# Both borders of the experts' stage: a first shared tile inside attention's tail, layer 1's first rows and products ahead of the stage's end

## The reference

```python
xn = layernorm(x)
x = x + attention(xn) + experts0(xn)        # 16 heads of 16, causal; then layer 0's experts
xn = layernorm(x)
x = x + recurrence(xn) + experts1(xn)       # layer 1

def experts0(x):                            # 8 routed experts (256 -> 352 -> 256), top 2, and a shared one
    expert = lambda x, w1, b1, w3, b3, w2, b2: silu((x @ w1 + b1) * (x @ w3 + b3)) @ w2 + b2
    scores = softmax(x @ gate_w.T)
    rw = the scores of the two best of scores + gate_b, zero elsewhere
    return sum over e of rw[:, e] * expert(x, expert e) + expert(x, shared)

def recurrence(x):
    z = sigmoid(x @ Wz + bz); h_tilde = x @ Wh + bh
    h[t] = (1 - z[t]) * h[t-1] + z[t] * h_tilde[t]
    return sigmoid(h @ Wg + bg) * h

def experts1(x):
    scores = sigmoid(x @ gate.T)            # two best of the better group, normalised
    lat = x @ fc1_w.T                       # width 128, 8 experts on it
    return fc2(sum over chosen e of score * relu2(lat @ w1[e].T) @ w2[e].T) + relu2(x @ up_w.T) @ down_w.T
```

## Time and profile before

| | |
|---|---|
| median of 3 runs | 1202.05 us (1201.46 to 1204.6) |
| the profiled execution | 1203.08 us, of it 1201.3 us span, 1.78 us around it |
| mean granted clock of the matrix engine | 0.979 |
| matrix engine busy | 1115.7 us (93%), 8899 instructions |
| VectorE busy | 894.9 us (74%) |
| ScalarE busy | 676.0 us (56%) |
| GpSimd busy | 531.2 us (44%) |

### The profile page before, as it was taken

One profiled execution on the slowest core, in us unless ns is written; L12 is line 12 of the kernel. 1 busy time (PEld: TensorE's weight loads), 2 busy tenths in 40 slices (PEclk: granted clock), 3 DMA queues, 4 the chain that ended last, 5 costly groups with the idle time before them and its releaser, 6 DMA issues. The chain is left out here.

```text
span 1201.3 us, 26766 instructions
## 1 busy us (share of the span) xinstructions
PE 1115.7 (93%) x8899; PEld 747.5 (62%) x8931; DVE 894.9 (74%) x2219; ACT 676.0 (56%) x1464; POOL 531.2 (44%) x743
## 2 busy tenths in 40 slices
PE   6799999999999888998999999997999999999998
PEld 3345555555555437887998888983656646546555
DVE  5878797888887847975656667674886876877876
ACT  2355565565555554665656566654654654664653
POOL 6442433434333226854444343323646546447414
PEclk9799999999999999999999999997999999999999
DMA  6448435455334405755332453452241341331211
GB/s 162 108 90 227 99 68 110 98 98 107 62 85 93 82 18 186 218 162 155 113 101 79 126 159 122 127 155 74 89 141 35 107 140 35 105 106 63 95 45 62
DMA packets 105044, 129.36 MB, mean 108 GB/s; under 512 B 14976, under 2 KB 92736, under 8 KB 103936
## 3 DMA queue, kind: packets, MB, share of 16 engines
q1 hardware_dynamic: 93712, 109.08, 34.1%
q0 software_dynamic: 6912, 18.88, 5.6%
q10 hardware_dynamic: 4336, 0.34, 0.3%
HBM read 84.70 MB, written 43.38 MB: 107 GB/s over the span
## 5 line engine op out<-in xcount | busy, mean ns | idle before, releaser
L544 ACT ACTIVATE p<-bank 128x384 f32<-128x384 f32 (+1 forms) x384 | 191.6, 531 | 185.2 <-PE bank L957 136.1
L769 DVE TENSOR_REDUCE neg_max<-bank 128x1 f16<-128x384 f32 (+3 forms) x352 | 219.7, 640 | 65.9 <-PE bank L945 56.5
L463 POOL TENSOR_SCALAR_AFFINE_SELECT p<-p 128x256 f32<-128x256 f32 x256 | 104.5, 412 | 233.8 <-ACT p L544 233.1
L942 PE MATMUL bank<-k_stack,q_stack 96*128 96x384 f16 (+3 forms) x512 | 133.2, 312 | 23.4 <-DVE neg_max L769 13.0
L1404 POOL DMA_INDIRECT fetched<-xn_dram,token_now x80 | 81.2, 1014 | 42.9 <-POOL token_now L1400 30.7
L2033 POOL TENSOR_TENSOR up_lo<-up_sq,up_hi 128x512 f16<-128x512 f32 x32 | 43.8, 1398 | 120.8 <-ACT up_hi L2090 120.8
L2044 POOL TENSOR_TENSOR he_lo<-he_sq,he_hi 128x512 f16<-128x512 f32 x64 | 79.9, 1270 | 36.6 <-ACT he_hi L2133 36.6
L957 PE MATMUL bank<-q_stack,k_stack 97*128 97x512 f16 (+1 forms) x256 | 91.5, 360 | 3.1 <-ACT p L544 1.5
L1488 ACT ACTIVATE a<-xbank,b 128x256 f32<-128x256 f32 (+1 forms) x126 | 58.7, 469 | 52.3 <-PE xbank L151 48.8
L1576 DVE TENSOR_TENSOR h_lo<-h,h_hi 128x256 f16<-128x256 f32 x159 | 68.0, 431 | 24.3 <-ACT h_hi L1497 23.4
L975 PE MATMUL bank<-p,v_aug 128*32 128x512 f32 (+3 forms) x1024 | 83.9, 447 | 0.8 <-DVE o_rows L749 0.8
(11 more groups left out here) (344 smaller groups left out, 3379.9 us busy)
## 6 DMA issues: line engine op xcount, KB each, us to landing
w_bc<-wT_dram SPq DMA_DIRECT2D x8, 2048.0 KB, 8.3
y_routed_dram<-y SPq DMA_DIRECT2D x37, 256.0 KB
w<-in_w SPq DMA_DIRECT2D x10, 704.0 KB
pack<-in_pack SPq DMA_DIRECT2D x12, 342.0 KB, 4.4
xr<-in_x SPq DMA_DIRECT2D x8, 512.0 KB, 6.9
xn_dram<-xn SPq DMA_DIRECT2D x8, 512.0 KB, 3.0
qk_hi_dram<-qk_hi SPq DMA_DIRECT2D x16, 256.0 KB, 2.7
qk_lo_dram<-qk_lo SPq DMA_DIRECT2D x16, 256.0 KB, 2.9
```

Source lines behind the costliest of these rows:

```text
L463: pool.affine_select(out=diagonal, in_=diagonal, pattern=[[0, 2], [1, P]], compare_op=ALU.is_ge, fill=0.0, base=0, channel_multiplier=-1). ...
L544: act.activation(p32[:, s // GH % 2, s % GH, cols], s_bank[n][:, 0:cols.stop - cols.start], ACT.Exp).then_inc(p_exp.sem, 1)
L769: dve.tensor_reduce(neg_max[:, g % 2, 0:GH * TT].rearrange("p (h t) -> p h t", t=TT)[:, heads[0]:heads[-1] + 1, j], a_bank[c % 2][:, 0:len ...
L942: pe.matmul(to[:, at * w:(at + 1) * w], q_stack[0:STK, u, h0 + h, j * P:(j + 1) * P], k_stack[0:STK, u, h0 + h, 0:w], start=at == 0, stop= ...
```

## The change

In the experts' stage, `HEAD_TILES` is 10 now and `TAIL_TILES` 6. The table is made after tile 7, and the parts of `pack` are 11 of 747 columns.

At attention's end: GpSimd's iotas run at step 14 of the last batch, VectorE's slot finding at its steps 26, 28, 30 and 32. The last group's `values` go to a bank of their own (`bank[3]`), straight behind those of the group before. The transposes of the first half of the output (c = 0) stand in step 40. Gate and up of the first shared tile for m = 0 and m = 1 (24 products) stand between the steps of the tail and behind it, so that in the stage tile 0 has only m = 2; ScalarE loads silu's table there. Buffers and banks are shared by the stages.

In the experts' stage: `pack_lo` is made by GpSimd, five parts ahead of its wait for the table, four after its last fetch and two after the gather of layer 1's first rows. At the end the first sums are made one stage earlier counted from the end's sixth tile, ScalarE normalises after stage 4's hidden values, and the transposes follow `out(4)` in stage 5. The new `tail` makes, before the border, the router's products, `lat` and `z0` of layer 1's first batch, the sigmoid and `lat_hi` on ScalarE, and GpSimd's gather for batch 1. Layer 1's three small loads (biases) are issued at the stage's start.

```diff
-TAIL_TILES = 5
+TAIL_TILES = 6
+PACKED_EARLY = 5
+AT_LAST_T, AT_NUMBERS, AT_SLOTS = 40, 14, (26, 28, 30, 32)
...
+        def out_of(g):
+            return bank[3] if g == GROUPS - 1 else out_bank
...
+            first_bias(0)
+            out_high(NB - 1, 1, last_t[1])
+            act.activation(silu_table[:, :], bq[:, 0:1], ACT.Silu)
...
+                    if b + 1 == NB:
+                        if at in AT_SLOTS:
+                            find_slots(AT_SLOTS.index(at))
+                        if at - 1 == AT_LAST_T:
+                            last_high()
+                            out_low(b, 0, last_t[0])
...
+                    elif at == AT_LAST_T:
+                        pe.wait_ge(x1_ready.sem, x1_ready.at(NB - 2))
+                        out_transposes(b, 0, last_t[0])
...
-            turn_out(GROUPS - 2)
+            pe.wait_ge(a_max.sem, a_max.at(GROUPS - 1))
             for ks in AT_VALUES.values():
                 values(GROUPS - 1, ks)
+            turn_out(GROUPS - 2)
+            first_tile(0, 0)
             turn_out(GROUPS - 1)
-            for c in range(DC):
-                out_transposes(NB - 1, c, last_t[c])
-            for g in range(2):
-                out_products(NB - 1, g, last_out[g])
+            first_tile(0, 1)
+            out_transposes(NB - 1, 1, last_t[1])
+            last_products(0)
+            last_products(1)
+            first_tile(1, 0)
+            first_tile(1, 1)
...
+            def pack_part(n):
+                cols = bass.ds(n * PACK_PART, PACK_PART)
+                pool.wait_ge(pack_hi_s.sem, pack_hi_s.at(n))
+                pool.tensor_tensor(pack_lo[:, cols], pack32[:, cols], pack_hi[:, cols], ALU.subtract).then_inc(pack_lo_s.sem, 1)
...
-            pool.wait_ge(slots.sem, slots.at(0))
...
+            for n in range(PACKED_EARLY):
+                pack_part(n)
             end = pool.value_load(bounds[0:1, E:E + 1], min_val=MIN_TILES, max_val=ROUTED_TILES)
...
+            for n in range(PACKED_EARLY, HEAD_TILES - 1):
+                pack_part(n)
             pool.wait_ge(front.slot_s.sem, front.slot_s.at(0))
...
+            for n in range(HEAD_TILES - 1, PACK_PARTS):
+                pack_part(n)
...
+            pool.wait_ge(front.x2_sum.sem, front.x2_sum.at(0))
+            pool.wait_ge(front.slot_s.sem, front.slot_s.at(1))
+            for t in range(TT):
+                for k in range(2):
+                    pool.indirect_dma_start(front.rows_k[:, t, k, :], None, dram["y_routed"], ...
...
-                if stage == TAIL_TILES - 1:
-                    first_normalise()
                 for m in range(HM):
                     hidden(i, m)
+                if stage == TAIL_TILES - 2:
+                    first_normalise()
+                if stage == TAIL_TILES - 1:
+                    first_x_high()
...
-                elif stage == TAIL_TILES - 3:
+                if stage == TAIL_TILES - 4:
                     first_sums(0)
                     first_sums(1)
-                elif stage == TAIL_TILES - 2:
+                elif stage == TAIL_TILES - 3:
                     first_sums(2)
                     first_sums(3)
...
-                gate_up(i, u, 0, n)
-                gate_up(i, u, 1, n)
+                if not is_int(i, 0):
+                    gate_up(i, u, 0, n)
+                    gate_up(i, u, 1, n)
...
+            def tail(i, u):
+                out(i, u)
+                first_products(i)
```

More of the change, by code:

```diff
@@ L195, in mix_phase @@
         xn = sb("xn", [P, TT, D])
[L196 removed]
+        xT_hi, xT_lo = (carried.xT[:, k] for k in range(2))
         qk_hi, qk_lo = (sb(f"qk_{k}", [P, 4, S], F16) for k in ("hi", "lo"))
@@ L224, in mix_phase @@
         tot = sb("tot", [P, 2, TT, E])
-        run = route["run"]
-        bank = [ps(f"bank{i}", [P, 512]) for i in range(8)]
+        run, bounds, pos, slots = route["run"], route["bounds"], route["pos"], carried.slots
+        steps, above, tiles, ends, starts = carried.steps, carried.above, carried.tiles, carried.ends, carried.starts
+        base, posf, pos_part = carried.base, carried.posf, carried.pos_part
+        bank = carried.bank
         w_loaded = sig("w_loaded", 16 * 8)
-        wqkv_hi_s = sig("wqkv_hi_s", DC)
-        wqkv_lo_s = sig("wqkv_lo_s", DC)
-        w_hi = sig("w_hi", 2)
-        w_lo = sig("w_lo", 2)
+        w_hi = sig("w_hi", 4)
+        w_lo = sig("w_lo", 4)
         bq_scaled = sig("bq_scaled", 1)
@@ L497, in _ @@
                             x_bias(b + 2)
+                    if b + 1 == NB and at == AT_NUMBERS:
+                        numbers()
         @block.scalar
@@ L2035, in step @@
             def step(b, u, before, more):
-                if more:
+                if before and more:
                     gather(b + 1)
```

408 lines of the change are left out of this document (245 added, 163 removed).

## The result

The changed kernel is slower: a median of 1210.17 us (1206.92 to 1214.27, 9 runs) against 1202.23 (1200.65 to 1205.65, 9 runs), ratio 1.0069 with a 95% interval of 1.0052 to 1.0086. The forecast was 1186.5, in a range of 1181.5 to 1193.

The account below looks back on a forecast made before the run. The matrix engine, 93% busy, was taken as the bound, with only idle and slow-clock time to win. Gains of 12.2 us (front) and 3.95 (end) made 16.2, giving 1186.9 profiled and a forecast of 1186.5, range 1181.5 to 1193.

Parts of the forecast that it names:

- Attention's tail: At attention's end: the experts' stage starts at 454.0, 2.2 us earlier, with 2.62 us of its products done.
- (a): Head of the experts' stage: GpSimd starts `in_lane` at once and is through 43.2 us after the border.
- (b): Head's shared tiles: 5.89 us each instead of about 6.5; PE then waits some 3.9 us ahead of the table.
- (d): Head's end: fetch and copy take 7.9 us; PE can transpose at 515.0, after waiting 1.6 us for rows.
- (c): GpSimd's five `pack_lo` parts ahead of the fetch: 1.85 us each, 9.25 together, making GpSimd late, not the table.
- The rival that had the lock in it: GpSimd and VectorE hold each other up in the head: five parts cost 14 us, total 1190 to 1192; chance 0.13.
- costs nothing elsewhere: In the head: taking `pack_lo` off VectorE has no cost elsewhere, as VectorE was the slower of the two there.
- The end up to the border: Experts' end: no 4.18 us wait for `l_xn`, `out(5)` at full clock from 820.0, products until 825.2.
- The border takes 1.0 us: Border between experts' stage and layer 1: PE resumes 1.0 us after its last products, at 826.2.
- The rows of batch 1: Layer 1's start: with the gather 10 us earlier, PE's two waits of 0.48 and about 0.8 go, gaining 1.2 us.
- The second: Rival: the clock falls again at a border or new wait; total 1189 to 1192 us, chance 0.13.
- The fifth: Rival: the 3.9 us wait before the table sets the clock low and it stays there; 1205 us, chance 0.03.

Follow-up runs that it names:

- packs_late: The changed kernel with GpSimd's five early `pack_lo` parts moved behind its last fetch: 1.0036 of the kernel before, 0.9995 in a second batch.
- mended_again: Second timing of the changed kernel with batch 1's gather back in layer 1, stores ahead of loads, early packs behind the last fetch: 1199.17 us, ratio 0.9973.
- gather_back: The changed kernel with only the gather of batch 1's rows moved back to layer 1's start: 1.0076 of the kernel before, 1.0057 in a second batch.
- rows_early: The changed kernel with stores ahead of loads, early packs behind the last fetch, batch 1's gather right behind batch 0's in its own buffer: 1194.85 us, ratio 0.9943.
- best_places: `rows_early` with weights over two tiles, batch 1's gather split around the statistics, VectorE making the last two packs, ten `place` pieces a tile: 1184.30 us, ratio 0.9847.

## Why the prediction was wrong

**Attention's tail: right.** The stage starts at 454.16 against 454.0, tile 0's 24 products lie where they were expected, and the slots cost attention nothing that shows.

**(a), the start of `in_lane`: right.** It begins 0.3 us into the stage and ends at 494.09, 39.9 us on, against 43.2.

**(b), the tiles' 5.89 us each: this step failed.** "a tile costs 5.89 (PE's own)" was worked out from PE and VectorE alone. Two things were not weighed. One is SyncE's queue: y has one buffer, its store has to land within one tile, and with tile 0 shortened the megabyte of weights was issued behind the moment when y was ready and ahead of its store. 5.91 us of waiting, and 477.6 to 481.8 at half clock, 2.1 us of work. The other is VectorE beside the packs: 4.07 us, and 503.6 to 509.1 at half clock, 2.8 us. A third low stretch, 516.2 to 519.4, came behind the forecast wait of 3.91 us, with 1.6 us. Together 16.5; the 1.6 us of waiting for `xg`, which (d) had, did not come: 14.9 of the 15.1 us by which 530.14 is later than 515.0.

**(c), the packs: near in the price, wrong in who pays.** A part took 1.6 us, under the bound of 1.70, so even the price was a little high. The estimate from the figure of the Trainium skill, "GPSIMD Engine Reference", section 3.1 Elementwise, was 1.6 too (for five parts it makes 8.1 us, not the prediction's 8.2), and the trace agrees with 8.03. GpSimd was through at 502.1 and then waited 19.54 us for `tokens`; it was not late. The rival that had the lock in it put its price on GpSimd's parts ("five parts at 2.8 us"), and it fell on VectorE, whose short pieces of `place` each took as long as the part beside them, 1.64 us. The sentence that what VectorE gives up "costs nothing elsewhere" is the one that `packs_late`, and the rows of `mended_again` at 770, refute.

**(d), fetch and copy: right.** 521.63 to 529.51, 7.9 us.

**The end up to the border: right.** From stage 4's start PE's `out(5)` was forecast at 15.2 us and stood at 15.5; the products ended at 825.4 (825.2), the gather ran from 816.0 to 825.8 (815.1 to 825.1), `l_xn` was not waited for.

**"The border takes 1.0 us": this step failed.** It was taken from the gap behind VectorE's last operation. GpSimd's close of the block, 7.3 us at the same border before, was hidden there, and no row of a busy view shows it; it was 7.9 now and began at 825.8 in place of 812.9. PE resumed 29.35 us behind stage 4's start instead of 21.4: 7.9 us. The gather was placed where it was the last work of the one engine whose close is long; in `gather_back` and `rows_early`, where GpSimd's last work ends at 820.1 and 810.9, its close is over before PE comes to the border, and the wait is gone.

**The rows of batch 1: half right.** VectorE's sums at 840.24 have no wait, and PE's 0.48 us behind them is gone. But its second wait, 0.82 for `up_sq` before, is there as before (0.83 at 851.05), so the forecast 1.2 us were 0.5.

15.1 + 7.9 = 23.0 us of misses. The way from the fetched rows to stage 4 took 3.0 us less than before (1.7 of it since the low stretch at 560 did not come), which leaves 20.0, and with the 0.8 us at batch 1's rows 20.8; the profiled run was 1207.92 against a forecast of 1186.9, 21.0. The direction was wrong since the forecast gain of 16.2 was smaller than these. `best_places` ends 18 us below the kernel before: with the three faults out, a gain of the forecast's size is there. That it has this size is not a proof of the forecast's sum, since the kernel has more than the faults taken out: buffers of their own for the early rows, a `place` that ends a tile sooner, a new order on GpSimd and two parts of `pack_lo` on VectorE.

**The rivals.** The second, the clock, came true as a follower of the new waits and not by itself. The fifth, slower than before, was put on a clock that stays low after the wait at the table; that did not happen (one stretch of 3.4 us), and neither the store's wait nor GpSimd's close was among the five.

## What to carry to other kernels

When work is taken out of one stretch, list what else has to happen in it: each load, store and single buffer that had the old time is a candidate for the next wait, the queue of the loading engine first. Before a last operation is moved in front of a block's end, look how long that engine takes to close the block, also in instructions that busy views leave out; on GpSimd it was 0.08 us for each indirect DMA of the whole block, so what counts is when its last work ends. And when elementwise work goes from VectorE to GpSimd, price it from VectorE's side: not only what it no longer does, but how long each of its operations on two SBUF operands will now take.

## What the runs showed of the hardware

GpSimd's DRAIN ended 0.06 us behind its last work in a block without indirect DMAs, 4.0 with 48 of them, 4.65 with 56, 7.3 with 88 and 7.9 with 96, that is 0.08 us for each, in all twenty traces. Fewer indirect DMAs for the same rows should by this shorten the close; no run here tried it. Short VectorE operations (`in_column`, 0.23 us each) took 1.64 us beside GpSimd subtractions of 1.6 us, and `h_lo` 1.8 in place of 0.42, while operations with an operand in PSUM kept 0.37 and 0.42. In three of the five batches of kernels, whose kernel before took 1239 to 1242 us instead of 1202 to 1204, ScalarE waited 7 to 9 us in six of layer 1's eight batches for something the trace calls remote, and the kernels had 3 to 15 us of such waits at the experts' end; nothing run here explains it.
